# Scan units begin behind the first MLP chunk of a step, not the third

## The chip, the cores and the metric

The kernel runs on one core of one Trainium2 chip. The metric is the device time of one execution in microseconds (us), taken as the median of several runs. Five engines work side by side, each through its own list of instructions in order: TensorE (PE, matmuls, with its weight loads PEld), VectorE (DVE), ScalarE (ACT), GpSimd (POOL) and SyncE (SP, which here only issues transfers). They wait for each other by semaphores.

## The reference

Eight samples of 256 tokens by 256 features pass three layers: half an expert layer, a Mamba block with its MLP, half an expert layer again.

```python
x = x + 0.5 * ffn(layernorm(x))          # 32 experts, top 6 of sigmoid scores, F=96, plus a shared one, F=192
x = x + attn(layernorm(x))               # Mamba mixer and MLP
x = x + 0.5 * ffn(layernorm(x))

# attn(h0):
h  = rmsnorm(h0, ln1_w)
z, x, B, C, dt = split(h @ in_proj_w.T)  # 512, 128, 128, 512, 128 columns
dt = softplus(dt @ dt_proj_w.T + dt_proj_b)
x  = silu(conv4(repeat(x)) + conv_b)
state[t] = exp(dt[t] * A) * state[t-1] + dt[t] * x[t] * B[t]   # 512 channels, 16 states each
y[t] = sum_over_states(state[t] * C[t])
h  = h0 + ((y + x * D_param) * silu(z)) @ out_proj_w.T
return h + (silu(h2 @ gate_w.T) * (h2 @ up_w.T)) @ down_w.T    # h2 = rmsnorm(h, ln2_w), 1024 inner
# ffn: every expert is computed for every token; its gated hidden is weighted by the router's combine weight
```

## The kernel before

Everything lies transposed, features on the 128 partitions, tokens along the free axis. The program is a chain of eleven steps, t = -1 to 9, a software pipeline over the samples. Step t holds the MLP of sample t - 2, the Mamba scan of sample t - 1 and the expert layers: the second one of a sample that has left the MLP, and the first one of a sample still to come, side by side in one pass of up to 512 columns. From t = 1 to 7 the scan of the next sample is also begun at the step's end, so that each of these steps starts its own scan at unit 6.

**Heavy work** is made of chunks of 128 hidden features.

- MLP, 8 chunks. `gum` is gate and up in one bank: L850, eight matmul rows in the trace (float32 matmuls show as two). ScalarE takes the tanh (L1051), VectorE gates (L1166) and multiplies (L1168), and `down` adds into the accumulator (L889).
- Experts, 26 chunks. `g` and `u` are L808 to L810, in split precision. Then come tanh (L1051) and the copy of `u` (L1041) on ScalarE, the gate `by_g` (L1175) on VectorE, the products `by_u` and `by_comb` on POOL (L1457, L1465), and `down` (L889). `cmb` (L862) broadcasts the combine weights of three chunks.
- The results of matmuls lie in three banks `gub`, used in turn.

**Light work** is the scan and what surrounds it. The scan has 32 units: 4 channel blocks of 8 pairs of states. The first half of a unit is `ub`: TensorE broadcasts B into a bank (L983), ScalarE makes the decays (L1139), VectorE multiplies by dt*x (L1340). The second half is `unit`: VectorE scans (L1352), TensorE broadcasts C (L986), VectorE multiplies by it (L1358), POOL sums (L1478). Both halves take a bank from a pool of three, `side`. So do the mean and variance matmuls (`n1`, `n2`: L906, L914), the router (`rt1`, L926), and the projections of the "front", which prepares the scan's inputs: `z`, `x`, `split` (L956) and `dt` (L967), with the convolution `xc`, `xd` (L1283, L1288), `sp` and `sp_dt` (L1318 to L1327) on VectorE. The first half of the channels has its front in the step before ("next"), the second in the scan's own step ("own"). `outp` (L996) is the output projection.

**Order.** No scheduler decides it. `items_of(t)` writes one list per step, and each engine walks it and does its part of every item. `merge(heavy, light, length)` interleaves two lists: each item gets a position in 0 to 1 by the sum of the weights ahead of it (`WEIGHT`: `gum` 1.7, `down` 1.7, `g` and `u` 1.3, `ub` and `unit` 2), and both lists are spread over the whole range. `near` pulls an item that frees a `side` bank forward where more than two others would take one ahead of it. VectorE and POOL walk the list in `late_order`, which puts some items back: a `unit` by one heavy item.

A matmul waits until the use three back of its bank has been read; an item `ub` three uses behind another waits for that one's scan. `keep` (L1222) copies the MLP result of the last sample to a buffer whose store must have landed; `again_a`, `b_rest` and `wl` are loads on SP's queue; `mg`, `md` load MLP weights from POOL's queue, each with a small paced operation (L1442) ahead of it.

For t = 2 to 6 the list is made by the last branch:

```python
heavy = mlp_items() + ahead + ff
out = hand + heavy[:6] + keep + fetches + merge(heavy[6:-TAIL], light, weight) + heavy[-TAIL:]
```

`hand` turns over the normalised inputs of the experts; `heavy[:6]` is `gum 0, mg 3, gum 1, mg 4, gum 2, mg 5`; `TAIL` is 6.

Of the kernel before, what the change touches and what calls it, by code (L numbers as in the profile page):

```python
# [162 lines left out]
def norm(which):  # L163
    centred = [] if which[:3] == "rms" else [("nc", which)]
    return [("n1", which)] + centred + [("n2", which), ("nm", which)]


def routing(call, when=()):
    return [("rt1", call) + when] + [("rq", call, i) + when for i in range(len(ROUTE))]


def unit_items(item, begin, end):

    out = []
    for u in range(begin, end):
        j, p = u // PAIRS, u % PAIRS
        out += [("ub", u, item), ("unit", u, item)]
        out += [("yz", j - 1)] if p == 2 and j else []
    return out
# [15 lines left out]
def after(items, new, *befores):  # L195
    at = max(items.index(b) for b in befores) + 1
    return items[:at] + new + items[at:]
# [7 lines left out]
def near(items):  # L205

    out, done, open_for = [], set(), {}

    def emit(it):
        if it in done:  # L210
            return
        if it[0] == "xd":
            emit(("xc",) + it[1:])
        fills = it[0] in FILLS and kind_of(it) != "n1r"
        if fills:
            for end in [e for e, n in open_for.items() if n >= SIDES - 1 and e != it]:
                emit(end)
            for end in open_for:
                open_for[end] += 1
        open_for.pop(it, None)  # L220
        done.add(it)
        out.append(it)
        if fills and it[0] in ENDS:
            open_for[(ENDS[it[0]],) + it[1:]] = 0

    for it in items:
        emit(it)
    return out
# [28 lines left out]
def items_of(t):  # L257


    if t < 0:  # L260
        ln1 = norm("ln1")
        return [("load", 0)] + ln1[:2] + [("load", 1)] + ln1[2:] + norm("ln1b")
    mamba, mlp = 0 <= t - 1 < BATCH, 0 <= t - 2 < BATCH


    own = OWN_SLOT.get(t)
    next_front = 1 <= t < BATCH
    ready = [slot for slot in ("f1", "f2") if slot != own and t <= BATCH]
    hand = [("hx", call) for call in ready]
    hand += [("rt2", call) for call in ready] if t else []  # L270
    keep = [("keep",)] if 3 <= t <= BATCH else []
    fetches = ([("again",), ("again_b",)] if t == 0 else [("again_a",), ("again_b",)] if t < 3 else
               [("again_a",)] if t in (3, 5) else [])
    turn = [("r0",), ("carry",)] if mamba else []
    turn += [("fetch",)] if next_front else []
    ln2 = norm("ln2") + routing("f2") if mlp and not own else []
    ln1 = norm("ln1") + routing("f1") if t in NORMED_IN else []
    fetches += [("load", 0)] if ln1 else []
    if t in NORMED_IN and len(NORMED_IN[t]) > 1:
        ln1 = ln1[:2] + [("load", 1)] + ln1[2:] + norm("ln1b") + routing("f2")  # L280
    ahead = [(k, c) for c in range(MSLOTS) for k in ("mgn", "mdn")] if 0 <= t + 1 - 2 < BATCH else []
    ff = ffn_items(t)
    if t == 0:
        early = [it for call in ("f1", "f2") for it in routing(call, ("early",)) + [("rt2", call)]]
        at = ff.index(("cmb", "ff", 0))
        return near(fetches + hand + merge(ff[:at], early, WEIGHT) +
                    merge(ff[at:-TAIL], ln1, WEIGHT) + ahead + ff[-TAIL:])
    chain = []
    if own:
        chain = (norm("ln2a") + routing("f1") if own == "f1" else norm("ln2") + routing("f2")) + [  # L290
            ("rt2", own), ("hx", own)]
        chain = mlp_items() + ahead + chain
        if not mamba:
            return chain + ff
    follow = norm("lnA") + norm("rms1") + merge(front(0, "next"), ln2, SPACE) if next_front else ln2
    light = norm("lnO") + norm("rmsO") + front(0, "own") if t == 1 else []
    begun = merge(unit_items(t - 1, 0 if t == 1 else LEAD, UNITS // 2), front(1, "own") + ln1, SPACE)
    light += begun
    units = unit_items(t - 1, UNITS // 2, UNITS)
    light += merge(units, follow, SPACE) if follow else units  # L300
    last = [("yz", JC - 1), ("outp",), ("om",)] + norm("rms2")
    light += merge(unit_items(t, 0, LEAD), last, SPACE) if next_front else last
    weight = WEIGHT if next_front else ENDING
    turns = [("end", "mlp")] if mlp else [("nm", "lnO")]
    if not mlp:
        out = fetches + hand + merge(ff[:-TAIL], light, weight) + ahead + ff[-TAIL:]
    elif own:
        cut = len(begun) * 2 // 3
        out = hand + keep + merge(chain, light[:cut], weight) + merge(ff[:-TAIL], light[cut:], weight) + ff[-TAIL:]
    else:  # L310
        heavy = mlp_items() + ahead + ff
        out = hand + heavy[:6] + keep + fetches + merge(heavy[6:-TAIL], light, weight) + heavy[-TAIL:]
    out = near(after(out, turn, *turns))
    if next_front:

        at = out.index
        assert at(("fetch",)) < at(("n1", "lnA")) and at(("ub", UNITS // 2, t - 1)) < at(("split", 0, "next"))
        assert at(("yz", 1)) < min(at(("xc", 0, "next")), at(("z", 0, "next")))
    if ln2:
        assert out.index(("end", "mlp")) < out.index(("n1", "ln2"))  # L320
    return out
# [16 lines left out]
TAIL = 6  # L338
# [3 lines left out]
def merge(heavy, light, length):  # L342


    def starts(items):
        at, out = 0.0, []
        for it in items:
            out.append(at)
            at += length.get(it, length.get(it[0], 0.1))
        return [x / at for x in out]  # L350

    both = [(x, 0, i, it) for i, (x, it) in enumerate(zip(starts(heavy), heavy))]
    both += [(x, 1, i, it) for i, (x, it) in enumerate(zip(starts(light), light))]
    return [b[3] for b in sorted(both, key=lambda b: b[:3])]


def mlp_items():
    out = []
    for p in range(MLP_CHUNKS + 2):
        if p < MLP_CHUNKS:  # L360
            out.append(("gum", "mlp", p))
            if p + MSLOTS < MLP_CHUNKS:
                out.append(("mg", p + MSLOTS))
        if p >= 2:
            out.append(("down", "mlp", p - 2))
            if p - 2 + MSLOTS < MLP_CHUNKS:
                out.append(("md", p - 2 + MSLOTS))
    return out + [("end", "mlp")]
# [7 lines left out]
def ffn_items(t):  # L376


    splits, more = t == 0, t + 1 < BATCH + 2
    out = []  # L380
    if splits:
        out += [("raw", c) for c in range(RAWS)] + [("ws", c) for c in range(WAHEAD)]
    for p in range(FFN_CHUNKS + DLAG):
        now, before = p < FFN_CHUNKS, 1 <= p <= FFN_CHUNKS

        late = t < 2 and p < 3
        out += [("cmb", "ff", p // 3)] if p < ROUTED and p % 3 == 0 and not late else []
        out += [("g", "ff", p)] if now else []
        out += [("by_u", "ff", p - 1)] if before else []
        out += [("by_comb", "ff", p - 1)] if 1 <= p <= ROUTED and not late else []  # L390
        out += [("down", "ff", p - DLAG)] if p >= DLAG else []
        out += [("by_g", "ff", p), ("u", "ff", p)] if now else []
        if late and p == 2:
            out += [("cmb", "ff", 0), ("by_comb", "ff", 0), ("by_comb", "ff", 1)]
        if splits:
            out += [("keep_w", p)] if now else []
            out += [("raw", p + RAWS)] if p + RAWS < FFN_CHUNKS else []
            out += [("ws", p + WAHEAD)] if p + WAHEAD < FFN_CHUNKS else []
        elif p + WSLOTS < FFN_CHUNKS:
            out += [("wl", p + WSLOTS)]  # L400
        if now and more and p == last_in(p % WSLOTS):
            out += [("wln", p % WSLOTS)]
    if t < BATCH - 1:
        out += [("end", "f1" if t == 0 else "f1n")]
    if t in (1, 2, 4, 6):
        out += [("store_a",)]
    if t < 3:
        out += [("end", "f1b"), ("store_b",)]
    if 3 <= t <= BATCH:
        out += [("end", "f2"), ("store",)]  # L410
    if t in OWN_SLOT:
        out += [("end", "f2a")]
    return out + ([("store_own",)] if t >= BATCH else [])
# [1150 lines left out]
```

## Time and profile before

| | |
|---|---|
| median of 3 runs | 1780.58 us (1778.83 to 1783.36) |
| profiled execution | 1783.27 us, span of its trace 1781.4 us |
| TensorE busy | 1551.8 us, 87% |
| VectorE busy | 1265.5 us, 71% |
| GpSimd busy | 988.8 us, 56% |
| ScalarE busy | 843.5 us, 47% |
| chain that ended last | TensorE 11%, VectorE 1%, rest of it unnamed |

The rows of the engines show how full each is over the whole span. They don't tell who waits for whom: for that the trace is cut by stretches of time. In it, the steps whose order changes begin at 401.72 (t = 2), 606.29 (t = 3), 785.11 (t = 4), 972.52 (t = 5) and 1151.87 us (t = 6), each with the transposes of L940; step 7 begins at 1331.58.

### The profile page before, as it was taken

The numbers are of one execution on the slowest core, as the hardware profiler recorded it, in microseconds if no ns is written. First come the engines' busy times: TensorE is split into PE (matmuls) and PEld (weight loads), VectorE is DVE, ScalarE is ACT, GpSimd is POOL, SyncE is SP. The second block draws the span as 40 slices with busy tenths as digits, with TensorE's granted clock in tenths as the row PEclk, the third lists the DMA queues.
The fourth block names the chain that finished last, engine by engine and source line by source line (L and its number), as shares of the span: only waits on it lengthen the run. The fifth ranks groups of instructions, "written<-read, shape, count | busy, mean of one in ns | idle before, by whom it ended". The sixth has DMA issues, their size and how long they took to land. (4 is left out here: it accounts for less than half of the span.)

```text
span 1781.4 us, 22496 instructions
## 1 busy us (share of the span) xinstructions
PE 1551.8 (87%) x7088; PEld 1165.3 (65%) x7088; DVE 1265.5 (71%) x2067; ACT 843.5 (47%) x1692; POOL 988.8 (56%) x1048
## 2 busy tenths in 40 slices
PE   5998887887899889888998799879987998889979
PEld 4665554546566567666776677667765776667868
DVE  4553587876868788968797879778977787777321
ACT  4443454543555346535553466346634564444323
POOL 1663354654767457636665566447644666458525
PEclk9999999999999999999999999999998999889989
DMA  4565221123323232423232333233322333233434
GB/s 161 205 217 192 75 95 50 63 77 103 133 90 113 97 121 92 138 88 116 95 126 96 98 115 128 89 104 116 126 95 73 124 114 113 80 112 131 133 100 149
DMA packets 73430, 202.35 MB, mean 114 GB/s; under 512 B 10049, under 2 KB 22561, under 8 KB 72929
## 3 DMA queue, kind: packets, MB, share of 16 engines
q1 hardware_dynamic: 65120, 175.75, 29.6%
q0 software_dynamic: 8192, 25.17, 4.6%
q8 instruction: 57, 0.93, 0.2%
q14 instruction: 61, 0.49, 0.1%
HBM read 175.46 MB, written 25.43 MB: 113 GB/s over the span
## 5 line engine op out<-in xcount | busy, mean ns | idle before, releaser
L1478 POOL TENSOR_TENSOR ring<-ring 128x512 f32<-128x512 f32 x192 | 256.9, 1338 | 378.9 <-DVE ring L1358 378.6
L808 PE MATMUL gub<-x_hi,wr 128*128 128x384 f32 (+2 forms) x1040 | 428.9, 412 | 29.1 <-DVE hid L1175 22.4
L889 PE MATMUL acc<-hid,w_down 128*128 128x384 f32 (+2 forms) x1040 | 408.1, 516 | 15.6 <-POOL hid L1457 15.5
L1457 POOL TENSOR_TENSOR hid<-hid,u_sb 128x384 f32<-128x384 f32 (+2 forms) x260 | 292.0, 1123 | 182.2 <-ACT u_sb L1041 168.0
L810 PE MATMUL gub<-x_hi,wr 128*128 128x384 f32 (+2 forms) x1040 | 370.0, 356 | 0.0
L809 PE MATMUL gub<-x_lo,wr 128*128 128x384 f32 (+2 forms) x1040 | 369.8, 356 | 0.0
L1352 DVE TENSOR_TENSOR_SCAN ring<-decays,side 128x512 f32<-128x512 f32 x256 | 310.4, 1213 | 40.1 <-ACT decays L1139 37.3
L1051 ACT ACTIVATE hid<-gub 128x384 f32<-128x384 f32 (+2 forms) x324 | 156.6, 483 | 365.9 <-PE gub L850 189.5
L1041 ACT ACTIVATE u_sb<-gub 128x384 f32<-128x384 f32 (+2 forms) x260 | 132.2, 508 | 336.6 <-PE gub L810 336.5
L1465 POOL TENSOR_TENSOR hid<-hid,weight 128x384 f32<-128x384 f32 (+2 forms) x240 | 267.6, 1116 | 29.6 <-ACT weight L1031 15.0
L889 PEld LDWEIGHTS acc<-hid,w_down 128*128 128x128 f32 x1040 | 185.7, 192 | 110.9 <-issue 41.8
L808 PEld LDWEIGHTS gub<-x_hi,wr 128*128 128x128 f32 x1040 | 202.1, 194 | 64.5 <-issue 37.4
L1340 DVE TENSOR_TENSOR side<-dtx,side 128x512 f32<-128x512 f32 x256 | 176.7, 690 | 93.5 <-PE side L983 93.1
L1139 ACT ACTIVATE decays<-dts,a_neg 128x255 f32<-128x255 f32 x512 | 228.5, 497 | 0.1
L809 PEld LDWEIGHTS gub<-x_lo,wr 128*128 128x128 f32 x1040 | 202.7, 195 | 20.0 <-issue 6.3
L810 PEld LDWEIGHTS gub<-x_hi,wr 128*128 128x128 f32 x1040 | 201.2, 193 | 13.8
L1175 DVE SCALAR_TENSOR_TENSOR hid<-hid,gub 128x384 f32<-128x384 f32 (+2 forms) x260 | 149.1, 573 | 85.7 <-ACT hid L1051 85.6
L1358 DVE TENSOR_TENSOR ring<-ring,side 128x512 f32<-128x512 f32 x256 | 176.2, 688 | 46.1 <-PE side L986 22.6
L983 PE MATMUL side<-bst,sel_b 96*128 96x256 bf16 x512 | 100.9, 279 | 63.4 <-DVE ring L1352 46.2
L850 PE MATMUL gub<-xn_mlp,wm_gu 128*128 128x256 f32 x512 | 129.3, 402 | 4.7 <-DMA wm_gu<-in_w_mlp 3.5
L956 PE MATMUL side<-rn,w_in 128*128 128x256 f32 x448 | 118.1, 411 | 15.5 <-DVE ring L1352 13.4
L983 PEld LDWEIGHTS side<-bst,sel_b 96*128 96x128 bf16 x512 | 40.3, 99 | 133.0 <-DVE ring L1352 62.0
(117 smaller groups left out, 1856.8 us busy)
## 6 DMA issues: line engine op xcount, KB each, us to landing
wr<-w_halves SPq DMA_DIRECT2D x234, 512.0 KB, 3.3
wm_gu<-in_w_mlp POOLq DMA_DIRECT2D x64, 256.0 KB, 3.1
w_halves<-wr SPq DMA_DIRECT2D x26, 512.0 KB, 3.2
wm_down<-in_w_mlp POOLq DMA_DIRECT2D x64, 128.0 KB, 2.7
w_raw<-in_w_gu SPq DMA_DIRECT2D x26, 256.0 KB, 3.7
rows<-parts SPq DMA_DIRECT2D x16, 384.0 KB, 2.3
cst<-rows SPq DMA_DIRECT2D x48, 128.0 KB, 2.5
xin<-in_x SPq DMA_DIRECT2D x8, 256.0 KB, 3.0
```

Of the source, the lines that this page charges most:

```text
L808: mm(out, w[:, 0, half, k, :], x_hi[:, k, a:b], start=(k == 0), stop=False)
L809: mm(out, w[:, 0, half, k, :], x_lo[:, k, a:b], start=False, stop=False)
L810: last = mm(out, w[:, 1, half, k, :], x_hi[:, k, a:b], start=False, stop=(k == KC - 1))
L889: last = mm(acc[k][:, a:b], w, h[:, a:b], start=(c == 0), stop=(c == (MLP_CHUNKS if mlp else FFN_CHUNKS) - 1))
L1051: A(hid[c % HSLOTS][:, a:b], s.gub_of(it)[:, a:b], ACT.Tanh, scale=0.5).then_inc(sem["tanh_done"], 1)
L1139: A(decay[u % 2][:, h, 1:SEQ], dts[:, j, 1:SEQ], ACT.Exp, scale=a_neg[:, j, n:n + 1]).then_inc(sem["decay"], 1)
L1340: v.tensor_tensor(b, twice(dtx[:, j, :]), b, ALU.mult).then_inc(sem["driven"], 1)
L1352: v.tensor_tensor_scan(w.rearrange("p h s -> p (h s)"), decay[u % 2][:, :, :].rearrange("p h s -> p (h s)"), s.side_of(ub)[:, :], 0.0, ALU ...
L1358: v.tensor_tensor(w, w, pair(s.side_of(it)), ALU.mult).then_inc(sem["read_out"], 1)
L1457: nc.gpsimd.tensor_tensor(h, h, u_sb[c % USLOTS][:, a:b], ALU.mult).then_inc(sem["hidden"], 1)
L1465: nc.gpsimd.tensor_tensor(h, h, weight[c // 3 % CSLOTS][:, a:b], ALU.mult).then_inc(sem["weighted"], 1)
L1478: add(ysum, ysum, ring[:, ring_at(it)], ALU.add).then_inc(sem["y_sum"], 1)
```

## The change

The fixed head of the list is `heavy[:2]`, that is `gum 0, mg 3`, and not `heavy[:6]`. `keep` and the loads of `fetches` follow behind it, and the merge with the light list starts there. The light list of these steps begins with the scan's units from 6 on and the front of the second half. The instructions are the same; steps -1, 0, 1, 7, 8 and 9 are made by other branches and stay.

```diff
     else:
         heavy = mlp_items() + ahead + ff
-        out = hand + heavy[:6] + keep + fetches + merge(heavy[6:-TAIL], light, weight) + heavy[-TAIL:]
+        out = hand + heavy[:2] + keep + fetches + merge(heavy[2:-TAIL], light, weight) + heavy[-TAIL:]
```

On TensorE the beginning of step 3, from its transposes on, was this (L850 is an MLP chunk of four matmuls, L889 its down product, L983 and L986 the B and C broadcasts, L956 the x projection):

```order
L940 MATMUL side<-ident,c_f 96x128 x3
L850 MATMUL gub<-xn_mlp,wm_gu 128x256 x12
L889 MATMUL acc<-hid,wm_down 128x256 x2
L983 MATMUL side<-bst,sel_b 128x256 x2
L956 MATMUL side<-rn,w_in 128x256 x4
L850 MATMUL gub<-xn_mlp,wm_gu 128x256 x4
L986 MATMUL side<-cst,sel_c 128x256 x2
L889 MATMUL acc<-hid,wm_down 128x256 x2
L983 MATMUL side<-bst,sel_b 128x256 x2
L850 MATMUL gub<-xn_mlp,wm_gu 128x256 x4
```

and is now:

```order
L940 MATMUL side<-ident,c_f 96x128 x3
L850 MATMUL gub<-xn_mlp,wm_gu 128x256 x8
L983 MATMUL side<-bst,sel_b 128x256 x2
L956 MATMUL side<-rn,w_in 128x256 x4
L850 MATMUL gub<-xn_mlp,wm_gu 128x256 x4
L986 MATMUL side<-cst,sel_c 128x256 x2
L889 MATMUL acc<-hid,wm_down 128x256 x2
L983 MATMUL side<-bst,sel_b 128x256 x2
L850 MATMUL gub<-xn_mlp,wm_gu 128x256 x4
```

Two chunks, not three, stand ahead of the first B broadcast, and the second one comes with one chunk and one down product less ahead of it. Two chunks and not one stand there since the merge's first places still go to the heavy list.

On VectorE the same step, where the MLP ends and the expert chunks begin, was this (L1340 the product with B of unit 11, L1205 and L1228 `end mlp` and `r0`, L1175 the gate `by_g 0`, L1352 and L1358 the scan and the product with C of unit 11, L1305 `sr 2`, L1325 and L1327 `sp_dt`, the last row `by_g 1`):

```order
L1340 TENSOR_TENSOR side<-dtx,side 128x512
L1205 SCALAR_TENSOR_TENSOR x<-acc,res 128x256 x2
L1228 TENSOR_TENSOR res<-x,hn_next 128x512
L1175 SCALAR_TENSOR_TENSOR hid<-hid,gub 128x384
L1352 SCALAR_TENSOR_TENSOR ring<-decays,side 128x512
L1358 TENSOR_TENSOR ring<-ring,side 128x512
L1305 TENSOR_TENSOR tmp<-side,parts 128x512
L1340 TENSOR_TENSOR side<-dtx,side 128x512
L1325 TENSOR_TENSOR dtx<-dtx,lbuf 128x512
L1327 TENSOR_TENSOR dts<-dtx,dts 128x512
L1175 SCALAR_TENSOR_TENSOR hid<-hid,gub 128x384
```

and is now, down to `by_g 0` and the scan of unit 12:

```order
L1340 TENSOR_TENSOR side<-dtx,side 128x512
L1352 SCALAR_TENSOR_TENSOR ring<-decays,side 128x512
L1358 TENSOR_TENSOR ring<-ring,side 128x512
L1305 TENSOR_TENSOR tmp<-side,parts 128x512
L1205 SCALAR_TENSOR_TENSOR x<-acc,res 128x256 x2
L1228 TENSOR_TENSOR res<-x,hn_next 128x512
L1340 TENSOR_TENSOR side<-dtx,side 128x512
L1325 TENSOR_TENSOR dtx<-dtx,lbuf 128x512
L1327 TENSOR_TENSOR dts<-dtx,dts 128x512
L1175 SCALAR_TENSOR_TENSOR hid<-hid,gub 128x384
L1352 SCALAR_TENSOR_TENSOR ring<-decays,side 128x512
```

Unit 11, `sr 2`, the product of unit 12 and `sp_dt` stood behind the gate of the first expert chunk, and stand ahead of it.

## Rows read from the trace of the kernel before

**Rows 1.** The page, part 1: busy us, share of the span, instructions.

```profile
PE 1551.8 (87%) x7088; PEld 1165.3 (65%) x7088; DVE 1265.5 (71%) x2067; ACT 843.5 (47%) x1692; POOL 988.8 (56%) x1048
```

**Rows 2.** Windows of steps 3 and 4: us, busy by engine, granted clock, DMA.

```profile
606.29:785.11 178.82, 156.69 (x763) 122.05 (x764) 143.16 (x223) 90.25 (x187) 108.76 (x119) 0.98 0.34 112
785.11:972.52 187.41, 162.94 (x780) 127.16 (x779) 150.37 (x247) 94.25 (x193) 105.95 (x118) 0.95 0.32 105
```

**Rows 3.** TensorE's waits from 606.3 to 656.3: us, times, longest.

```profile
PE side L956 <- DVE ring L1352: 2.6, 1, 2.6
PE side L986 <- DVE xs L1288: 2.4, 1, 2.4
PE side L983 <- DVE ring L1352: 2.4, 2, 1.4
PE gub L808 <- DVE hid L1175: 2.1, 2, 1.6
```

**Rows 4.** VectorE's timeline in step 3: start, us, instruction, idle before it.

```profile
613.65 0.69 DVE L1340 TENSOR_TENSOR side<-dtx,side 128x512 f32<-128x512 f32 x1
617.06 0.42 DVE L1166 SCALAR_TENSOR_TENSOR hid<-hid,gub 128x256 f32<-128x256 f32 x1 [2.72 <-ACT hid L1051]
...
617.86 1.21 DVE L1352 TENSOR_TENSOR_SCAN ring<-decays,side 128x512 f32<-128x512 f32 x1
...
628.81 0.42 DVE L1166 SCALAR_TENSOR_TENSOR hid<-hid,gub 128x256 f32<-128x256 f32 x1 [2.40 <-ACT hid L1051]
...
646.64 0.55 DVE L1175 SCALAR_TENSOR_TENSOR hid<-hid,gub 128x384 f32<-128x384 f32 x1 [2.30 <-ACT hid L1051]
...
652.40 0.54 DVE L1175 SCALAR_TENSOR_TENSOR hid<-hid,gub 128x384 f32<-128x384 f32 x1
```

**Rows 5.** TensorE's timeline in step 3.

```profile
619.13 0.39 PE L983 MATMUL side<-bst,sel_b 96*128 96x256 bf16 x2 [1.43 <-DVE ring L1352]
619.36 1.89 PE L850 MATMUL gub<-xn_mlp,wm_gu 128*128 128x256 f32 x8
621.09 1.03 PE L889 MATMUL acc<-hid,wm_down 128*128 128x256 f32 x4
...
624.83 3.53 PE L850 MATMUL gub<-xn_mlp,wm_gu 128*128 128x256 f32 x8
...
641.21 3.26 PE L956 MATMUL side<-rn,w_in 128*128 128x256 f32 x8 [2.56 <-DVE ring L1352]
...
648.38 0.39 PE L983 MATMUL side<-bst,sel_b 96*128 96x256 bf16 x2 [1.00 <-DVE ring L1352]
```

**Rows 6.** Windows of step 3 behind its first 50 us.

```profile
656.29:721.29 65.00, 62.00 (x312) 48.24 (x312) 51.69 (x74) 41.29 (x83) 44.22 (x42) 1.00 0.36 122
721.29:767.29 46.00, 40.28 (x205) 31.52 (x204) 42.00 (x68) 21.08 (x47) 30.37 (x27) 1.00 0.33 110
```

**Rows 7.** A store's issue in step 3; transfers: count, KB each, us to landing.

```profile
607.54 0.32 SPq L782 DMA_DIRECT2D x_kept<-x2kept  x1
...
x_kept<-x2kept SPq DMA_DIRECT2D x3, 256.0 KB, 3.1
wm_gu<-in_w_mlp POOLq DMA_DIRECT2D x64, 256.0 KB, 3.1
```

**Rows 8.** TensorE's wait in step 2; wait and B broadcast in step 4.

```profile
PE gub L850 <- DMA wm_gu<-in_w_mlp: 3.5, 1, 3.5
...
PE side L926 <- DVE ring L1352: 1.5, 1, 1.5
...
832.70 0.39 PE L983 MATMUL side<-bst,sel_b 96*128 96x256 bf16 x2
```

**Rows 9.** Window of the MLP chunk that began at 624.83.

```profile
624.83:628.36 3.53, 3.53 (x12) 2.66 (x11) 1.48 (x2) 0.00 (x0) 1.78 (x2) 0.53 0.01 2
```

**Rows 10.** L1327 over the whole trace: ns min/median/max.

```profile
L1327 DVE TENSOR_TENSOR dts<-dtx,dts x16: 692/1640/1657, 199.5 to 1569.0; 128x512 f32<-128x512 f32 x16
```

## The prediction

> **What bounds the kernel now.** I read the page first: TensorE (PE) is busy 87% of the span and VectorE (DVE) 71% [rows 1]. Neither share says where the time goes, so I next cut out two of the five steps whose order changes, with the busy time of each engine [rows 2]. The reader should see that TensorE is short of full in both: it is idle for 178.82 - 156.69 = 22.1 us of the one and 187.41 - 162.94 = 24.5 us of the other. What it waits for stands in the table of waits of one such step's first 50 us [rows 3]: 2.6 + 2.4 + 2.4 + 2.1 = 9.5 us, each released by a VectorE instruction (a scan L1352, a convolution L1288, a gate L1175). So TensorE carries most of the work, and what can be won is the time that it stands behind VectorE in the shared in-order lists.
>
> Why VectorE is late there is in its own timeline [rows 4]. From 613.65 on it runs nearly without a break, but in the first 11 us of the step it has little to do: it stands 2.72 us before the gate at 617.06, then 2.40 us (628.81) and 2.30 us (646.64), each time for an activation of ScalarE that itself waited for a matmul. Once busy, it makes TensorE stand: 1.43 us before the B broadcast at 619.13, 2.4 us behind a convolution, 2.56 us before the C projection, 1.00 us before the B broadcast at 648.38, and twice before expert chunks, 2.1 us together [rows 3, 5]. After that comes a stretch of 65 us in which TensorE is 62.00 us busy, then one of 46 us in which VectorE is busy 42.00 and TensorE 40.28, then the step's end [rows 6].
>
> **The change, part by part.** Nothing is added or removed; the order of steps t = 2 to 6 alone changes. Two MLP chunks (`gum` 1 and 2, two `mg` loads) leave the fixed head and go into the merge. The light list therefore starts two chunks earlier; since both lists are spread over the whole merge, the lead shrinks to nothing at the step's end. A chunk is 1.73 us of TensorE (eight matmuls from 619.36, the next begins 621.09), so its down product of four is 0.86 [rows 5], its two gate operations 0.8 us of VectorE [rows 4].
>
> I follow the step that begins at 606.29, times from there, row durations kept, each operation started when its inputs by these orders are there.
>
> 1. First scan. The copy of L1222 comes ahead of chunk 1's gates: 0.33 us, in a place where VectorE waited anyway, so nothing. It waits for the last store of the step before: issued 607.54, landing after 3.1 us, at 4.35 [rows 7], while VectorE gets there at 4.06; 0.3 us, absorbed by the next gate's wait. The first B product goes from 7.36 to 5.5. Chunk 2 now runs behind the B broadcast (0.22) and the x projection (1.73), ends at 7.6 instead of 5.6, and its gates, 0.6 us behind it as at 617.06, stand ahead of the scan: they end at 9.1. Scan at 9.1 instead of 11.57: light work is 2.5 us ahead. But VectorE still waits 2 us before that gate, in place of the 2.72.
> 2. Next bank. TensorE comes to the second B broadcast at 8.65 and gets the bank at 10.3: waits 1.7 us, was 1.43. It is there 2.5 us earlier with one chunk and one down product (2.6 us) less done. Even.
> 3. Convolution. Its second half ends at 15.7 instead of 18.2; TensorE waits for it 2.7 us, was 2.4, again with 2.6 us of chunk work left over. Even. The half-clock stretch that follows (624.83: eight matmuls in 3.53 us, others 1.89) I keep, as its wait is kept.
> 4. Between the MLP and the expert chunks the order differs most: `by_g 0` now stands behind unit 11, sr 2, ub 12 and sp_dt. These are 1.9 + 0.6 + 0.6 + 2.2 = 5.3 us of VectorE, and they fill its 2.30 us wait. At the end of that gate VectorE is at 43.1; in the old list the same work is done at 652.40 = 46.1. It leads by 3.0 us.
> 5. TensorE does not get all of that. Its wait of 2.56 us before the C projection (L956 at 641.21) and the half-clock stretch behind it (3.26 us for eight matmuls) I keep. The B broadcast of unit 13 needs the scan of unit 12, which is behind the gate of point 4: bank free at 44.4, TensorE there at 42.4, a wait of 2.0 us. The old waits in this part are 3.1 us: 1.00 before the B broadcast at 648.38, and the 2.1 of L1175. At 44.6 TensorE has u 1 and g 2 (2.3 us) still to do, so it stands as at 46.9, where the old one stood at 45.9: 1.0 behind. The 2.1 us of L1175 mostly still lay ahead in the old list and now fall away, since VectorE leads: 1.1 us ahead by this count when unit 14 is reached. Counted by waits it is 9.5 - (1.7 + 2.7 + 2.6 + 2.0) = 0.5. I take the middle, **0.8 us**.
>
> The steps at 972.5 and 1151.9 have the same lists there or nearly so: 3 x 0.8 = 2.4 us. In the step at 785.1 (and, apart from its opening wait of 3.5 us for a weight load, which stays, that at 401.7) the same walk gives waits of about 1.7, 1.2, 0.8, 0.4, 1.5 and 2.5 us up to unit 12: scan of unit 11 behind the gate of expert chunk 0, at 43.8, with 2.3 us of chunk work left over, so TensorE is as at 46.2, where it stood at 47.6 before (B broadcast at 832.70, [rows 8]): 1.4 us early. The wait of 1.5 us before the router product L926 [rows 8] should shrink by some 0.6: 2.0 us each, 4.0 together.
>
> In the 46 us stretch VectorE is nearly full. The lists enter it with about one light piece more done (0.69 us of VectorE, L1340's) and leave it at the same place, so the wait there shrinks by about 0.6 us: 3.0 in five steps. I take nothing from the 65 us stretch, which has no waits to give back, nor from the step's end, where the two orders are the same.
>
> SP's queue: `again_a` and `b_rest` pass two chunks on which they do not wait; POOL's: `mg` 4 and 5 and `md` 3 issue later behind the first units' sums, but with 3.1 us to landing [rows 7] and over 6 us until their chunk. Nothing. Without that cover a late load costs TensorE up to 3.5 us, as at the step of 401.7 [rows 8].
>
> **Sum:** 2.4 + 4.0 + 3.0 = 9.4 us. The profiled run took 1783.27 us with a span of 1781.4; it lies 2.7 above the median 1780.58. From it I get 1773.9; from the median, which is what is compared, **1771.2 us**.
>
> Bounds. Below: all of VectorE's 3.0 us lead reaches TensorE in every step, and the nearly full stretch gives 1.3: 5 x 4.3 = 21.5, to 1759. Above: the unit-13 wait is not repaid (step 5 stays at 1 us behind) and nothing comes later: 1780.6 + 5 = 1786.
>
> TensorE's clock: right behind the 2.4 us wait the granted clock is 0.53 over 624.83 to 628.36 [rows 9]; a chunk takes 3.53 us instead of 1.89 [rows 5]. That is 1.2 GHz against 2.4, a price of 1.64 us. The 2.0 us wait of point 5, which replaces three smaller ones, may bring one such stretch more in each step: 8.2 us in five, and 1779.4 in place of 1771.2. I keep their number, since the waits of 1.43 and 1.00 us brought none. The Trainium skill, "TensorE: Matmul & The Clock Gate", Part 1, says that idleness brings the half rate back; by it the longer wait is the dearer one.
>
> Port: L1327, with both inputs in SBUF, takes 0.69 to 1.66 us, median 1.64 [rows 10]. Moving it to where POOL works or does not can cost or save 0.95 us a step, 4.8 in all; I take it unchanged at 1.39. The Trainium skill, "SBUF — State Buffer", "Who interferes with whom", says that such an instruction contends with GpSimd's reads, by an exclusive lock. The rule gives no sign for the move.
>
> **Rivals.**
> *No gain (1775 to 1786, about 1780), 0.25.* VectorE's lead is handed back: points 2 and 3 come out even by my own walk, the middle stretch has nothing to give, and the half-clock stretch of point 5 comes (1779.4). For it: 62.00 busy of 65. Against it: the 2.30 us wait of VectorE really is filled.
>
> *Slower (about 1794), 0.18.* `by_g 0` behind 5.3 us of light work. The gate frees the bank of u 1 and lets POOL and the down products go on. If end mlp, r0 and these come 2 us later than I walk, the unit-13 wait is 4.0 and not 2.0, with a half-clock stretch of 1.64 behind it; 2.0 - 0.8 + 1.64 = 2.8 us a step behind the old order, and 5 x 2.8 = 14: 1794. It decides once VectorE's gate of expert chunk 0 starts over 44 us after the step's begin (42.6 by the walk). For it: VectorE's list there is full. Against it: the lead of 2.5 us that it brings.
>
> *Larger gain (1763 and under), 0.09.* Shorter waits also let half-clock stretches go. Granted clocks of 0.98 and 0.95 in two of the steps [rows 2] mean 2 x 0.02 x 178.82 = 7 us and 2 x 0.05 x 187.41 = 19 us at half clock, so there are stretches to lose; one fewer in each step saves 5 x 1.64 = 8.2 more: 1763.
>
> **How the numbers follow.** The forecast, 1763 to 1775, has 0.48. Faster by over 0.3% (5.3 us; about what can be told from no change) is below 1775.2: 0.57. Within: 0.25. Slower: 0.18. The range 1758 to 1788 leaves out most of the slower case (0.15) and the end of the larger gain (0.04), under 2 in 10.
>
> **What would show it.** In the changed profile, step of 606: the first scan about 9 us after the step's begin, not 11.6; VectorE's wait of 2.30 us before the first L1175 gone; TensorE's waits in the first 50 us still 8 to 10 us, with one of about 2.0 before an L983; the step 1 to 2 us shorter than 178.82; the 46 us stretch a little shorter. The prediction is wrong if new waits on L1175 stand in the 65 us stretch, which I take as full, or if the granted clock of the five steps moves by 0.01 or more.

## The result, and the profile after

The changed kernel takes 1769.94 us (median of 5, 1767.04 to 1770.33), the kernel before on the same chip 1778.83 us (1777.38 to 1783.36). The ratio is 0.9934, 95% interval 0.9910 to 0.9957: faster by 0.7%, about 11.7 us by the ratio (8.9 by the two medians). The forecast was 9.4 us and 1771.2. The profiled run of the changed kernel has a span of 1765.2 us. The two profiled runs lie 16.2 us apart: the one before (1783.27 us) is at the slow end of its kernel's runs, the one after (1767.04) is the fastest of its own. 5.5 us of this lie where the lists are the same (3.9 ahead of step 2, 1.6 behind step 6), so the traces are compared step by step and not by their spans.

The page, part 1, of the changed kernel, beside [rows 1]:

```profile
PE 1545.0 (88%) x7088; PEld 1158.0 (66%) x7088; DVE 1263.8 (72%) x2067; ACT 844.6 (48%) x1692; POOL 988.3 (56%) x1048
```

The windows of the five changed steps (t = 2 to 6) in the changed kernel; columns as in [rows 2]:

```profile
397.79:602.96 205.17, 188.17 (x781) 128.47 (x780) 156.07 (x246) 101.42 (x193) 124.05 (x129) 0.98 0.32 105
602.96:777.76 174.80, 154.77 (x763) 120.63 (x764) 141.70 (x223) 90.38 (x187) 108.90 (x119) 0.99 0.35 114
777.76:968.91 191.15, 166.72 (x781) 129.73 (x779) 150.36 (x247) 94.44 (x193) 105.40 (x118) 0.94 0.31 103
968.91:1145.58 176.67, 157.54 (x764) 122.40 (x764) 141.75 (x223) 90.40 (x187) 108.59 (x119) 0.97 0.34 113
1145.58:1316.97 171.39, 153.63 (x764) 119.88 (x763) 143.54 (x223) 90.36 (x187) 105.71 (x118) 1.00 0.35 113
sum 919.18, PE 820.84 PEld 621.11 DVE 733.42 ACT 467.00 POOL 552.65; mean PE 164.17 PEld 124.22 DVE 146.68 ACT 93.40 POOL 110.53
```

And of the kernel before:

```profile
401.72:606.29 204.57, 186.29 (x781) 127.64 (x780) 155.57 (x246) 101.25 (x193) 125.01 (x129) 0.98 0.32 105
...
1151.87:1331.58 179.71, 159.69 (x765) 124.79 (x763) 142.94 (x224) 90.21 (x187) 104.34 (x118) 0.96 0.34 108
sum 929.86, PE 822.90 PEld 623.91 DVE 735.15 ACT 466.21 POOL 552.77; mean PE 164.58 PEld 124.78 DVE 147.03 ACT 93.24 POOL 110.55
```

The reader should read these rows in two parts. The window minus TensorE's busy time is TensorE's **idle** time: 106.96 us before, 98.34 after, 8.6 less. TensorE's **busy** time is for the same matmuls and moves with the granted clock: 822.90 before, 820.84 after, 2.1 less. Together that is the 10.7 us by which the five steps are shorter. By steps it is +0.6, -4.0, +3.7, -2.7 and -8.3 us. The step at 1145.58 shows why the two must be kept apart: 2.3 us of its 8.3 are idle time, 6.1 are busy time, at a granted clock of 1.00 instead of 0.96. The step at 777.76 has no more idle time than before (24.43 for 24.47) and is 3.7 us longer at 0.94 instead of 0.95 [rows 2].

TensorE's waits in the first 50 us of step 3 of the changed kernel, beside [rows 3]:

```profile
PE side L956 <- DVE ring L1352: 2.6, 1, 2.6
PE side L986 <- DVE xs L1288: 2.4, 1, 2.4
PE side L983 <- DVE ring L1352: 1.4, 1, 1.4
PE side L940 <- DVE ring L1358: 1.1, 1, 1.1
PE gub L808 <- ACT weight L1031: 0.9, 1, 0.9
PE gub L808 <- DVE hid L1175: 0.6, 2, 0.4
```

The big waits of the MLP part are still there, unchanged to 0.1 us. The wait of L940 at the step's first instruction was 1.1 us before too. What went is the second wait of L983 (1.0 us) and most of the wait of L808 behind the gate L1175 (2.1, now 0.6), 2.5 us together. A wait of 0.9 us for ScalarE's L1031 is new and takes a part of it back. VectorE's timeline shows how, beside [rows 4]:

```profile
611.94 1.21 DVE L1352 TENSOR_TENSOR_SCAN ring<-decays,side 128x512 f32<-128x512 f32 x1
...
621.20 0.42 DVE L1166 SCALAR_TENSOR_TENSOR hid<-hid,gub 128x256 f32<-128x256 f32 x1 [0.71 <-ACT hid L1051]
...
642.65 0.69 DVE L1327 TENSOR_TENSOR dts<-dtx,dts 128x512 f32<-128x512 f32 x1
643.26 0.55 DVE L1175 SCALAR_TENSOR_TENSOR hid<-hid,gub 128x384 f32<-128x384 f32 x1
643.73 1.21 DVE L1352 TENSOR_TENSOR_SCAN ring<-decays,side 128x512 f32<-128x512 f32 x1
```

The step begins at 602.96. The first scan is at 8.98 (11.57 before), and the gate of the first expert chunk at 643.26 has no idle time ahead of it, where it had 2.30 us. It ends at 40.8 us of the step; before, the same list of VectorE work ended at 46.1.

### The profile page after: what moved, and what is told of

It is laid out like the page before. It is cut to its first block and busy times, and to the rows that moved or that the text cites. A ratio compares the mean times of both kernels' runs of the same rounds, so it can differ in the third digit from the quotient of the medians.

```text
span 1765.2 us, 22496 instructions
## 1 busy us (share of the span) xinstructions
PE 1545.0 (88%) x7088; PEld 1158.0 (66%) x7088; DVE 1263.8 (72%) x2067; ACT 844.6 (48%) x1692; POOL 988.3 (56%) x1048
## 5 line engine op out<-in xcount | busy, mean ns | idle before, releaser
L808 PE MATMUL gub<-x_hi,wr 128*128 128x384 f32 (+2 forms) x1040 | 423.4, 407 | 26.3 <-DVE hid L1175 17.4
L889 PE MATMUL acc<-hid,w_down 128*128 128x384 f32 (+2 forms) x1040 | 407.0, 515 | 15.5 <-POOL hid L1457 15.4
L1352 DVE TENSOR_TENSOR_SCAN ring<-decays,side 128x512 f32<-128x512 f32 x256 | 310.2, 1212 | 37.8 <-ACT decays L1139 35.0
L889 PEld LDWEIGHTS acc<-hid,w_down 128*128 128x128 f32 x1040 | 186.4, 192 | 111.4 <-issue 41.6
L808 PEld LDWEIGHTS gub<-x_hi,wr 128*128 128x128 f32 x1040 | 200.4, 193 | 61.2 <-issue 34.6
L1340 DVE TENSOR_TENSOR side<-dtx,side 128x512 f32<-128x512 f32 x256 | 176.6, 690 | 84.6 <-PE side L983 84.2
L1175 DVE SCALAR_TENSOR_TENSOR hid<-hid,gub 128x384 f32<-128x384 f32 (+2 forms) x260 | 148.9, 573 | 83.8 <-ACT hid L1051 83.5
L1358 DVE TENSOR_TENSOR ring<-ring,side 128x512 f32<-128x512 f32 x256 | 176.0, 688 | 41.8 <-PE side L986 17.7
L983 PE MATMUL side<-bst,sel_b 96*128 96x256 bf16 x512 | 101.7, 281 | 59.6 <-DVE ring L1352 42.8
L850 PE MATMUL gub<-xn_mlp,wm_gu 128*128 128x256 f32 x512 | 127.3, 395 | 4.8 <-DMA wm_gu<-in_w_mlp 3.8
L956 PE MATMUL side<-rn,w_in 128*128 128x256 f32 x448 | 116.0, 405 | 16.7 <-DVE ring L1352 14.4
L983 PEld LDWEIGHTS side<-bst,sel_b 96*128 96x128 bf16 x512 | 40.6, 100 | 129.0 <-DVE ring L1352 60.7
```

Of the source, the lines that this page charges most:

```text
L808: mm(out, w[:, 0, half, k, :], x_hi[:, k, a:b], start=(k == 0), stop=False)
L889: last = mm(acc[k][:, a:b], w, h[:, a:b], start=(c == 0), stop=(c == (MLP_CHUNKS if mlp else FFN_CHUNKS) - 1))
L1340: v.tensor_tensor(b, twice(dtx[:, j, :]), b, ALU.mult).then_inc(sem["driven"], 1)
L1352: v.tensor_tensor_scan(w.rearrange("p h s -> p (h s)"), decay[u % 2][:, :, :].rearrange("p h s -> p (h s)"), s.side_of(ub)[:, :], 0.0, ALU ...
L1358: v.tensor_tensor(w, w, pair(s.side_of(it)), ALU.mult).then_inc(sem["read_out"], 1)
```

## The experiments

The profiles were read in the same two parts, as sums over the five changed steps. "Head" is how many items stand ahead of the merge. The ratio is of several runs; steps, idle and busy time are of one profiled run each, which can lie at an end of them: that of "gate order alone" (1770.74 us) is the fastest of twelve, which go up to 1784.52; that of "head 2 in steps 3, 5, 6" (1772.07) is the slowest of six, and that of "head 4" (1777.23) nearly the slowest of seven.

| kernel | ratio to before (95%) | steps, us | idle | busy |
|---|---|---|---|---|
| before, head 6 | | 929.86 | 106.96 | 822.90 |
| changed, head 2 | 0.9934 (0.9910-0.9957) | 919.18 | 98.34 | 820.84 |
| changed, again | 0.9939 (0.9912-0.9966) | 919.35 | 98.82 | 820.53 |
| head 2 in steps 3, 5, 6 | 0.9907 (0.9880-0.9934) | 917.80 | 100.91 | 816.89 |
| head 2 in steps 2, 4 | 0.9989 (0.9970-1.0007) | 930.30 | 106.16 | 824.14 |
| gate order alone | 0.9975 (0.9957-0.9993) | 920.96 | 103.27 | 817.69 |
| gate order undone | 0.9984 (0.9971-0.9998) | 926.92 | 107.88 | 819.04 |
| head 4 | 0.9964 (0.9949-0.9978) | 925.69 | 96.70 | 828.99 |
| head 0 | 0.9886 (0.9871-0.9901) | 910.92 | 96.46 | 814.46 |
| copy and loads alone | 1.0011 (0.9998-1.0025) | 932.14 | 106.42 | 825.72 |
| head by step | 0.9872 (0.9843-0.9900) | 912.29 | 92.50 | 819.79 |
| head 0, again | 0.9879 (0.9851-0.9907) | 910.86 | 97.68 | 813.18 |
| changed, load ahead of sum | 0.9918 (0.9898-0.9939) | 914.39 | 98.83 | 815.56 |

The expectations speak of two theories, made after the first profiles. By theory A the gain comes from light work that fills VectorE's wait at the first expert gate. By theory B it comes from the earlier start of the light list, in every step.

**The changed kernel again.** No edit.

> The changed kernel once more, for a second profile of it. Both theories: 0.991 to 0.996 of the kernel before. The first profiles gave for the five changed steps +0.6, -4.0, +3.7, -2.7 and -8.3 us (t = 2 to 6). If these are the order's own, a second profile repeats each within 1 us; if the half-clock stretches decide them, t = 4 and t = 6 move by one or more stretches of 1.6 us while the waits of TensorE stay as they were.

Each step came out within 0.7 us of the first profile: 205.66, 175.23, 190.46, 176.60 and 171.40 us. So most of a step's length, half-clock time included, came back in a second execution. That this holds for every execution is not shown: the seven runs of this kernel go from 1767.88 to 1776.38 us, and only one of them was profiled.

**The change in some steps only.**

```diff
-        out = hand + heavy[:6] + keep + fetches + merge(heavy[6:-TAIL], light, weight) + heavy[-TAIL:]
+        head = 2 if t in (3, 5, 6) else 6
+        out = hand + heavy[:head] + keep + fetches + merge(heavy[head:-TAIL], light, weight) + heavy[-TAIL:]
```

> The change in steps 3, 5 and 6 alone (their lists have no routing of the first layer's next sample behind the MLP). Theory A, the gate theory: the gain is VectorE's wait before the first expert gate, filled by light work; by the first profiles these three steps carry -15.0 us and the other two cost 4.3, so this version reaches 0.990 to 0.993, 1761 to 1766 us, and beats the changed kernel. Theory B, the start theory of the prediction's sum (each step gains about 2 us, steps 2 and 4 the most): 2.4 + 1.8 = 4.2 us, 0.9976.

The other kernel has `head = 2 if t in (2, 4) else 6`.

> The change in steps 2 and 4 alone. Theory A: +4 us or no change, 1.000 to 1.003. Theory B: 4.0 + 1.2 = 5.2 us faster, 0.997.

Steps 3, 5 and 6 alone give 0.9907, steps 2 and 4 alone 0.9989, which is no change that can be told. Idle time says the same: 6.0 us less with the first, 0.8 with the second. Theory B, on whose walk the sum of the prediction stood, had it about even. Theory A also expected the first of these to beat the changed kernel. That isn't shown: their intervals overlap (0.9880 to 0.9934 and 0.9910 to 0.9957), and the changed kernel has 2.6 us less idle time.

**The gate order alone, in the old list.**

```diff
+    if t in (3, 5, 6):
+        early = ([("split", 2, "own")] if t == 6 else []) + [("unit", 11, t - 1), ("sr", 2, "own"), ("ub", 12, t - 1), ("sp_dt", 1, "own")]
+        out = [it for it in out if it not in early]
+        at = out.index(("cmb", "ff", 0))
+        out = out[:at] + early + out[at:]
```

> The old order in all steps, with only these items of steps 3, 5 and 6 moved ahead of the first expert chunk: unit 11, sr 2, the product of unit 12, sp_dt (in step 6 the projection that sr needs too). Theory A: VectorE's wait of 2.3 us before the first gate goes, about 2 us a step, 0.9965 to 0.998. Theory B, that the early start of the light list is what pays: nothing or a loss, since without the lead VectorE reaches the gate about 3 us later, 0.999 to 1.003.

0.9975 (0.9957 to 0.9993), in the range of theory A; the end of the interval just reaches the range of B, 0.999 and more. In the three steps idle time falls from 64.21 to 59.11 us (windows 180.00, 178.72 and 173.80 us long, TensorE busy 159.03, 157.86 and 156.52). The full change takes it to 56.92. So 5.1 of its 7.3 us of idle time there come with the order at the gate and need no lead; TensorE's busy time in the three steps is that of before (473.4 us for 473.7), so the two idle times can be compared. By the runs it is less: 0.25% for the order alone, 0.93% for the change in the same steps. The changed kernel has 7.7 us less busy time there as well, and no experiment says why. The first 50 us of step 3 of this kernel (it has five lines more in front of these, L961 is L956 of before, L813 is L808):

```profile
PE side L961 <- DVE ring L1357: 2.6, 1, 2.6
PE side L991 <- DVE xs L1293: 2.4, 1, 2.4
PE side L988 <- DVE ring L1357: 2.0, 2, 1.4
...
PE gub L813 <- DVE hid L1180: 0.7, 1, 0.7
PE gub L813 <- ACT weight L1036: 0.7, 1, 0.7
```

The wait behind the gate fell from 2.1 to 0.7 us, as in the changed kernel.

This kernel also shows that idle time is not quite free of the clock. Its step 4 has the list of before, but 26.05 us of idle time for 24.47, with 157.77 us busy for 162.94 [rows 2]:

```profile
780.76:964.58 183.82, 157.77 (x780) 124.00 (x779) 151.49 (x247) 94.34 (x193) 106.27 (x118) 0.98 0.33 107
```

Of the 5.2 us by which TensorE was faster, 1.6 came back as waiting.

**The gate order undone, in the new list.**

```diff
+    if t in (3, 5, 6):
+        back = [("unit", 11, t - 1), ("sr", 2, "own"), ("ub", 12, t - 1), ("sp_dt", 1, "own")]
+        out = [it for it in out if it not in back]
+        at = out.index(("g", "ff", 0)) + 1
+        out = out[:at] + back[:1] + out[at:]
+        at = out.index(("u", "ff", 0)) + 1
+        out = out[:at] + back[1:3] + out[at:]
+        at = out.index(("g", "ff", 1)) + 1
+        out = out[:at] + back[3:] + out[at:]
```

> The changed list, but in steps 3, 5 and 6 unit 11, sr 2, the product of unit 12 and sp_dt go back behind the first expert chunk (unit 11 behind g 0, sr 2 and the product of unit 12 behind u 0, sp_dt behind g 1). Theory A: VectorE's wait before the first gate is back, now with the later units queued behind these pieces as well; TensorE's waits in these three steps rise by 5 us or more against the changed kernel, and the ratio to the kernel before is 0.997 to 1.000. Theory B (the early start of the light list pays by itself): the ratio stays at 0.993 to 0.995.

0.9984. Idle time of the three steps goes from 56.92 to 65.38 us, 8.5 more, more than the change had won there. VectorE's wait is back, though not ahead of the first gate as expected (0.2 us there) but ahead of `end mlp`, which is L1214 here:

```profile
638.09 0.76 DVE L1214 SCALAR_TENSOR_TENSOR x<-acc,res 128x256 f32<-128x256 f32 x2 [2.79 <-PE acc L898]
```

Both directions agree: with the lead but without the order at the gate the gain in idle time is gone. But this edit isn't a clean inverse. L1327 (L1336 here) stands in a new place with it and takes 1.66, 1.64 and 1.66 us in the three steps, against 0.69 in each in the changed kernel. In step 3 it runs beside a sum of GpSimd:

```profile
647.06 1.66 DVE L1336 TENSOR_TENSOR dts<-dtx,dts 128x512 f32<-128x512 f32 x1
646.50 1.67 POOL L1487 TENSOR_TENSOR ring<-ring 128x512 f32<-128x512 f32 x1 [2.83 <-DVE ring L1367]
```

That is 2.9 us of VectorE's time that the order itself doesn't explain; how much of it reached TensorE was not tried apart. So the two experiments show that the order at the gate is what most of the idle time won in these steps hangs on, and leave open how much the faster L1327 and the lead add.

**Other heads.** `heavy[:4]` and `heavy[4:-TAIL]`:

> The light list begins behind the second MLP chunk (head of 4 items). Theory A: in steps 3, 5 and 6 three of the four light pieces already stand ahead of the first expert gate (unit 11, sr 2, the product of unit 12), so TensorE's waits there fall nearly as far as in the changed kernel, by 4 to 6 us; 0.994 to 0.997. Theory B: half of the changed kernel's gain, 0.997.

`heavy[:0]` and `heavy[0:-TAIL]`:

> The light list begins at once, ahead of the first MLP chunk's load (head of 0 items). Theory A: the pieces ahead of the first expert gate are those of the changed kernel, so there is no further gain, 0.992 to 0.996, unless VectorE meets the first B product before the handed-over inputs are ready. Theory B: one chunk more of lead gives some 40% more gain, 0.990 to 0.992.

Head 4 has less idle time than the changed kernel (96.70), but in its profile TensorE is busy 8.2 us longer with the same matmuls. By the runs it looks slower (0.9964), though the intervals overlap. Its idle time fell by 4.1 us in steps 3, 5 and 6, as theory A has it, and by 6.1 in steps 2 and 4, which no theory had. Head 0 beat both expectations. It has 1.9 us less idle time than the changed kernel, where theory A had none and theory B some 3.4 (40% of 8.6); the other 6.4 us of its steps are busy time, which neither theory had.

**The copy and the loads alone.**

```diff
+        out = hand + heavy[:2] + keep + fetches + heavy[2:6] + merge(heavy[6:-TAIL], light, weight) + heavy[-TAIL:]
```

> Only keep and the loads move ahead of MLP chunks 1 and 2, the merge is the old one. Both theories: no change, 0.999 to 1.001; the copy L1222 is then at most 0.3 us late for its store. If it is faster or slower by more than 0.2%, the sum left out a term.

1.0011, with an interval that takes in 1, and 106.42 us of idle time for 106.96. The copy and the loads cost nothing that can be told, as forecast.

**A head for each step.** `head = 0 if t in (3, 5) else 4`.

> Head of 0 items in steps 3 and 5, of 4 items in steps 2, 4 and 6: each step takes the head with which TensorE's waits in it were shortest in the profiles so far (14.2, 19.1, 19.7, 19.0, 16.2 us). If the waits belong to a step's own list, they come out as these within 0.5 us each, 88 us in sum against 93.6 with head 0 everywhere and 95.2 in the changed kernel; with equal half-clock time this is 0.985 to 0.988. If the half-clock time decides, the sum of waits holds and the time does not: 0.988 to 0.995.

The waits in this expectation are gaps of over 0.1 us between TensorE's instructions, some 4 us less in the five steps than the idle time of the windows. By that count the steps came out at 14.0, 19.2, 19.6, 19.2 and 16.2 us, 88.2 in sum: each within 0.2 us of the number on record. So here the waits belonged to a step's own list and added up; the step 4 of the order alone, above, is the exception seen. This version has the lowest ratio found: 1758.19 us, 0.9872. Its step 4 is 3.4 us longer than with head 0 (184.70), though it has 3.8 us less idle time, since TensorE is busy 7.2 us longer, at 0.94:

```profile
773.04:961.14 188.10, 166.79 (x780) 129.06 (x779) 149.48 (x247) 94.39 (x193) 104.62 (x118) 0.94 0.32 105
961.14:1133.99 172.85, 153.67 (x763) 119.67 (x764) 142.55 (x223) 90.11 (x187) 109.02 (x119) 1.00 0.36 115
```

**Head 0 again.**

> Head of 0 items in all five steps once more, on the same chip as the version before it. The first time gave 0.9886. Waits as before, 93.6 us in the five steps; 0.987 to 0.990. If its gain over the changed kernel (0.9939) was half-clock time that falls otherwise from run to run, it comes back as 0.991 or more.

0.9879: it repeats, with 97.68 us of idle time for 96.46. The interval is 0.9851 to 0.9907, so it can't be told from the head by step.

**The load ahead of the sum.** In the changed kernel's step 4 a new wait stands in the table of TensorE's waits from 777.7 to 825:

```profile
PE side L983 <- DVE ring L1352: 4.3, 3, 2.6
PE acc L889 <- DMA wm_down<-in_w_mlp: 1.9, 1, 1.9
PE side L967 <- DVE xs L1288: 1.2, 1, 1.2
```

POOL's timeline tells why the weights are late: the load (814.79) is queued behind a sum that stands 10.25 us for VectorE.

```profile
812.61 1.64 POOL L1475 TENSOR_TENSOR ring<-ring 128x512 f32<-128x512 f32 x1 [10.25 <-DVE ring L1358]
814.21 0.63 POOL L1442 TENSOR_TENSOR pool_pace<-eps_col 128x1 f32<-128x1 f32 x1
814.79 0.57 POOL L1448 DMA_DIRECT2D wm_down<-in_w_mlp  x1
```

The edit puts it ahead again, on POOL alone:

```diff
-    return out + ([held] if held is not None else [])
+    out += [held] if held is not None else []
+    for unit in (("unit", 9, 1), ("unit", 9, 3)):
+        if unit in out and ("md", 7) in out and ("gum", "mlp", 0) in out:
+            out.remove(("md", 7))
+            out.insert(out.index(unit), ("md", 7))
+    return out
```

> The changed kernel, with POOL issuing the load of the last MLP down weights (md 7) ahead of unit 9's sum in steps 2 and 4, as it did before the change. In the changed kernel this load queued behind the sum, which stood 10.25 us for VectorE, and TensorE stood 1.92 us for the weights in step 4 and 0.94 us in step 2. If that is the cause, both waits go, TensorE's idle time in the two steps falls by up to 2.9 us (less what the next wait takes back), and the ratio is 0.992 to 0.994. If the waits were VectorE's in truth, an L983 takes their place and the idle time stays.

The wait for the load is gone in both steps, and longer waits of L983 took its place. The same table, from 776.6 to 824 (five lines more ahead):

```profile
PE side L988 <- DVE ring L1357: 5.4, 3, 2.6
PE side L972 <- DVE xs L1293: 1.2, 1, 1.2
PE acc L894 <- DVE hid L1173: 0.3, 1, 0.3
```

Idle time stays: 98.83 for 98.34 us. The late load was real but covered waits for VectorE of nearly its size. The time (0.9918) is within the interval of the changed kernel.

## Why the prediction was right, and where only by its sum

The mechanism was right: VectorE's wait ahead of the first expert gate is filled with light work, TensorE's waits behind that gate shrink. The total was right too, 9.4 us forecast, 8.6 us of idle time and 11.7 us by the runs. Its split was not: steps 3, 5 and 6 were forecast at 4.2 us and won 7.3 us of idle time, steps 2 and 4 at 5.2 us and won 1.3. That the sum came out so near is in good part luck.

*The reading of VectorE's timeline.* It says that VectorE runs nearly without a break from 613.65 on. Its own rows say otherwise: the waits of 2.72, 2.40 and 2.30 us all lie behind that point [rows 4]. Nothing in the sum hangs on it.

*Points 1 to 3 (first scan, next bank, convolution).* Right. Scan at 8.98 (forecast 9.1). TensorE waits 1.43 and 2.43 us there (1.7 and 2.7), with the chunk work left over: even.

*Points 3 and 5, the half-clock stretches "I keep".* Wrong in this profile. The chunk behind the same 2.43 us wait took 1.89 us, not 3.53, and VectorE's wait for it was 0.71, not 2.40:

```profile
618.62 0.39 PE L986 MATMUL side<-cst,sel_c 96*128 96x256 bf16 x2 [2.43 <-DVE xs L1288]
618.85 1.89 PE L850 MATMUL gub<-xn_mlp,wm_gu 128*128 128x256 f32 x8
...
635.23 1.99 PE L956 MATMUL side<-rn,w_in 128*128 128x256 f32 x8 [2.56 <-DVE ring L1352]
```

The other one went too: behind the same 2.56 us wait the C projection took 1.99 us, not 3.26 [rows 5]. The granted clock of the first 50 us is 1.00, where it was 0.93. Later in the step a little of it came back, 0.96 from 717.96 to 760.54 where it had been 1.00 [rows 6].

*Point 4 (the gate).* Right in kind, too small: a lead of 5.3 us, not 3.0. By the rows, 1.7 us more are VectorE's shorter wait at 621.20, with the half-clock stretch gone, and 0.7 is L1327.

*The port.* L1327 was taken at 1.39 us and took 0.69 in its new place. Before, it ran beside a product of GpSimd:

```profile
651.08 1.39 DVE L1327 TENSOR_TENSOR dts<-dtx,dts 128x512 f32<-128x512 f32 x1
650.47 1.46 POOL L1457 TENSOR_TENSOR hid<-hid,u_sb 128x384 f32<-128x384 f32 x1
```

Now GpSimd issues weight loads at that time, with their paced operations. In step 5 it is again 1.39 before and 0.69 after; in step 6 it took 0.69 already. So the move saved 0.7 us of VectorE in two steps. Over the whole trace the median is still 1.64 us.

*Point 5 (B broadcast of unit 13).* **The step that failed.** I let it wait for the scan of unit 12. Counting the uses of `side` in the new list (unit 11, ub 12, unit 12, ub 13), the bank three back is that of unit 11, which had been read at 639. The row has no idle time, although the scan of unit 12 began only at 643.73:

```profile
643.23 0.39 PE L983 MATMUL side<-bst,sel_b 96*128 96x256 bf16 x2
```

In the old list the projection `split` stands between the B broadcasts of units 11 and 12, which made the second of them wait for the scan of unit 11, just ahead of it; I carried that distance over. So the wait of 2.0 us was not there, and the term of 0.8 us a step was too small: in step 3 the first 50 us have 8.0 us of idle time for 9.6, 1.6 less. With the late part, 2.4 + 1.8 = 4.2 us were forecast for steps 3, 5 and 6, and 7.3 us of idle time were won.

*Steps 2 and 4.* **The other step that failed.** The term of 4.0 us (5.2 with the late part) was too large: 1.3 us of idle time, all of it in step 2. In the first 50 us of step 4 the waits of L983 fell from 6.1 to 4.3 us, but the load's 1.9 us came in. The walk stopped at unit 12 and gave back 0.6 us of the router's wait (L926). In fact that wait went whole, and one of L983 with it, and TensorE then stood nearly as long behind the gates of later expert chunks, which the walk did not reach. From 840 to 870 before:

```profile
PE side L983 <- DVE ring L1352: 2.7, 1, 2.7
PE side L926 <- DVE ring L1352: 1.5, 1, 1.5
```

and in the changed kernel:

```profile
PE gub L808 <- DVE hid L1175: 3.4, 2, 1.9
```

Why these gates come late was not looked into. The two errors, of steps 3, 5 and 6 and of steps 2 and 4, nearly cancel.

*SP's and POOL's queues.* "Nothing" was wrong as a cost of the load: `md` 7, not the loads that I named, came to stand behind unit 9's sum. It costs no time of its own, as the last experiment shows.

*The 46 us stretch.* Neither term nor stretch can be settled apart: in step 3 its successor, and the 65 us one, show 3.3 and 4.9 us of idle time for 5.7 and 3.0:

```profile
652.96:717.96 65.00, 60.06 (x303) 46.68 (x301) 52.72 (x74) 44.62 (x88) 44.30 (x41) 1.00 0.38 124
717.96:760.54 42.58, 39.31 (x193) 30.82 (x194) 36.17 (x62) 16.22 (x37) 27.33 (x25) 0.96 0.34 106
```

These are cut at other places of the list than before, so the sum alone compares: 8.2 for 8.7.

*The rivals.* "No gain" needed the lead handed back and a half-clock stretch behind the wait of point 5; that wait didn't come. "Slower" needed the gate later than 44 us; it was at 40.3. "Larger gain" by fewer half-clock stretches came true in step 6 (6.1 us less busy time) and was undone in step 4 (3.8 more).

*The signs named ahead.* First scan and VectorE's wait came as forecast, and TensorE's waits in the first 50 us are 7.9 us, 9.0 with L940, for 8 to 10; the wait of about 2.0 us before an L983 did not, and step 3 is 4.0 us shorter, not 1 to 2 (2.1 idle, 1.9 busy). Of the two signs of being wrong, new waits on L1175 in the 65 us stretch are absent in step 3 but stand in step 4, as above. The other, a granted clock that moves by 0.01 or more, is met in four of the five steps (0.98 to 0.99, 0.95 to 0.94, 0.98 to 0.97, 0.96 to 1.00). It cost the sum little because these moves nearly cancel: over the five steps together the clock is 0.97 in both. That is luck too.

## What to carry to other kernels

In a kernel of hand-merged in-order lists, look for the engine that feeds the busiest one and stands idle right ahead of an item of the next phase, and move work across that border: here four or five items in each of three steps won 5.1 of the 7.3 us of idle time that a shift of the whole list won there. With rotating buffers, count the uses again in the new order before writing down who waits for whom. Then read a reordering in idle and busy time of the busiest engine, segment by segment, and tune each segment by itself: in the head by step these waits came out within 0.2 us and added up. Keep the measured time as the judge all the same: in step 6, and from head 2 to head 0, more of the gain was busy time, through the granted clock, than idle time, and in the order alone a faster TensorE waited more.

## What the runs showed of the hardware

The same list takes different times as its granted clock differs. Step 7 has the same list in all kernels. Its window in the kernel before:

```profile
1331.58:1516.00 184.42, 159.69 (x763) 123.95 (x764) 139.11 (x223) 90.79 (x187) 107.28 (x119) 0.94 0.33 107
```

And in the kernel with the change in steps 3, 5 and 6 only:

```profile
1318.36:1505.30 186.94, 162.95 (x764) 126.49 (x763) 139.01 (x223) 90.85 (x187) 106.98 (x119) 0.92 0.33 105
```

Busy time is 3.3 us more, at 0.92 for 0.94. In the five changed steps it ranges from 813.18 to 828.99 us over the kernels, 16 us for the same matmuls, more than the change itself; two profiles of one kernel agreed within 1.3 us. A wait of 2.4 us before the same broadcast was followed by eight matmuls in 3.53 us at a granted clock of 0.53, the level of 1.2 GHz, in the kernel before [rows 5, 9], and in 1.89 us at 1.00, 2.4 GHz, in the changed one. The Trainium skill, "TensorE: Matmul & The Clock Gate", Part 1, says that the window by which the clock is set runs freely, and that the point at which the clock changes depends on where in it the first matmul lands. The traces fit that, since unchanged steps behind a changed one came out with other clocks, as step 7 above; no run here shows the window itself. What decides it in each case was not tried.

VectorE's L1327, a 128x512 `TENSOR_TENSOR`, took 0.69 us where GpSimd only issued loads and did their paced operations, 1.39 us beside a product of GpSimd, and 1.66 us beside a sum of GpSimd. On GpSimd's queue a load stands behind the sum ahead of it in the list: 10.25 us of that sum's wait made a load of 814.79 late, and TensorE stood 1.92 us for it.
